# Weight quantisation moved from the second feed-forward into six slots of the first attention

## The reference, cut to what matters

```python
x = x + 0.5 * L0_ffn(layernorm(x))
x = x + L0_attn(layernorm(x))       # 16 heads of 8, banded bias
x = x + 0.5 * L0_ffn(layernorm(x))
x = x + 0.5 * L1_ffn(layernorm(x))  # FP4: the weights w_gate, w_up, w_down are quantised
x = x + L1_attn(layernorm(x))
x = x + 0.5 * L1_ffn(layernorm(x))

def fp4_quant_dequant(x):           # blocks of 16 along the last dimension
    scale = max(abs(block)) / 6
    q = nearest_grid_value(abs(x / scale)) * sign(x) * scale
```

## Time and profile before

| | |
|---|---|
| median of 3 runs | 506.68 us (506.49 to 509.33) |
| the profiled execution's own time | 506.44 us |
| its span in the profile | 504.6 us |
| PE busy | 418.7 us (83%) |
| DVE busy | 350.3 us (69%) |
| ACT busy | 285.1 us (56%) |
| POOL busy | 305.0 us (60%) |
| mean granted clock of TensorE | 0.91 |

### The profile page before, as it was taken

The page is one execution under the profiler, slowest core; times in us unless marked ns, Lnnn a source line. Parts: engine busy times, 40 slices in busy tenths (PEclk is TensorE's granted clock), DMA queues, the critical chain, the costliest instruction groups (busy, mean ns, idle before and its releaser), DMA issues.

```text
span 504.6 us, 11467 instructions
## 1 busy us (share of the span) xinstructions
PE 418.7 (83%) x3693; PEld 268.9 (53%) x3693; DVE 350.3 (69%) x882; ACT 285.1 (56%) x521; POOL 305.0 (60%) x585
## 2 busy tenths in 40 slices
PE   3996889999999967685788478799999998767975
PEld 1453425666666643343456355567766765334654
DVE  5769686888778644874899637857676776148992
ACT  5774515666666755657885135235455546668741
POOL 5314336777777770546898325346666677679961
PEclk9999957999999999987999679759999999579997
DMA  6001793332333000000000004973323330000001
GB/s 196 1 2 47 173 271 82 96 97 76 85 82 96 5 2 0 2 0 1 1 1 2 1 0 136 254 182 91 86 78 89 95 97 3 2 2 0 22 21 43
DMA packets 31122, 31.77 MB, mean 63 GB/s; under 512 B 4954, under 2 KB 26330, under 8 KB 31075
## 3 DMA queue, kind: packets, MB, share of 16 engines
q1 hardware_dynamic: 31074, 31.18, 23.2%
HBM read 21.30 MB, written 9.44 MB: 61 GB/s over the span
## 4 chain that ended last, share of the span: by engine, by line
PE 53%; DVE 14%; POOL 13%; issue 10%; ACT 6%; DMA 2%; SPq 1%; DVEq 0%; POOLq 0%; ACTq 0%
PE psum L639 6%; PE psum L293 4%; POOL hq L1175 4%; PE psum L593 3%; PE psum L623 3%; POOL hb_v L1170 3%; PE psum L594 2%; PE psum L596 2%; DVE nm L729 2%; PE psum L613 2%; PE psum L643 2%; DVE nm L732 2%; DVE xn L228 2%; PE psum L614 2%; PE psum L416 2%
## 5 line engine op out<-in xcount | busy, mean ns | idle before, releaser
L688 ACT ACTIVATE h_sb<-psum 128x1024 f32<-128x1024 f32 (+1 forms) x128 | 110.7, 914 | 52.8 <-PE psum L614 26.8
L729 DVE TENSOR_REDUCE nm<-psum 128x2 f32<-128x512 f32 x128 | 82.3, 685 | 14.0 <-PE psum L594 12.8
L732 DVE TENSOR_REDUCE nm<-psum 128x3 f32<-128x384 f32 x128 | 65.7, 552 | 11.3 <-PE psum L600 9.3
L698 POOL TENSOR_TENSOR h_sb<-h_sb,bandw 128x512 f32<-128x512 f32 x48 | 61.0, 1270 | 0.0
L234 POOL TENSOR_TENSOR rstd<-veps,mhalf 128x4 f32<-128x4 f32 (+1 forms) x32 | 28.3, 884 | 45.0 <-DVE veps L220 43.6
L639 PE MATMUL psum<-h_sb,v_b 128*32 128x256 f32 x512 | 44.0, 416 | 4.2 <-POOL h_sb L698 4.1
L766 DVE RECIPROCAL rsum<-psum 128x16 f32<-128x16 f32 x32 | 8.2, 258 | 49.7 <-PE psum L655 49.7
L702 POOL TENSOR_SCALAR_AFFINE_SELECT h_sb<-h_sb 128x512 f32<-128x512 f32 x64 | 40.8, 638 | 0.0
L593 PE MATMUL psum<-kst,qst 72*128 72x256 bf16 x128 | 36.0, 298 | 3.4 <-DVE nm L729 2.5
L596 PE MATMUL psum<-kst,qst 72*128 72x128 bf16 x128 | 30.2, 236 | 7.8 <-DVE nm L732 6.5
L594 PE MATMUL psum<-kst,qst 72*128 72x256 bf16 x128 | 36.1, 298 | 0.0
(11 more groups left out here) (234 smaller groups left out, 1158.3 us busy)
## 6 DMA issues: line engine op xcount, KB each, us to landing
qst<-q_dram SPq DMA_DIRECT2D x96, 96.0 KB
kst<-k_dram SPq DMA_DIRECT2D x96, 96.0 KB
q_dram<-q_parts SPq DMA_DIRECT2D x16, 192.0 KB, 3.2
k_dram<-k_parts SPq DMA_DIRECT2D x16, 192.0 KB, 3.5
k_dram<-k_parts SPq DMA_DIRECT2D x16, 128.0 KB, 3.6
x<-in_L_attn_x SPq DMA_DIRECT2D x4, 256.0 KB, 4.5
out_x<-x SPq DMA_DIRECT2D x4, 256.0 KB, 2.3
pk<-in_packed SPq DMA_DIRECT2D x1, 689.5 KB, 5.8
```

The costliest lines, as they stand in the source:

```text
L688: nc.scalar.activation(pexp[p][:, :, 0:w], psum[:, 4 + 2 * (p % 2):6 + 2 * (p % 2), 0:w], ACT.Exp, scale=scale).then_inc(sem("a_exp"), 1)
L698: ins = nc.gpsimd.tensor_tensor(wide, wide, bandw[:].unsqueeze(1).unsqueeze(1).to_broadcast([P, 2, 2, P]), ALU.mult)
L729: nc.vector.tensor_reduce(nm[slot % 2][:, HEAD[h]], bank[e].rearrange("p (t k) -> p t k", t=2), AX.X, ALU.max, negate=True).then_inc(sem(" ...
L732: nc.vector.tensor_reduce(nm3[slot % 2][:, HEAD[h]], bank[e][:, 0:3 * P].rearrange("p (t k) -> p t k", t=3), AX.X, ALU.max, negate=True).t ...
```

## The change

The entry `quantise` of `ffn_b` becomes empty. `unit` gets a hook that is called at its beginning, after DVE's second pair of maxima, and at its end. In the opening quad the hook handles matrices 0 and 1, in slots 0 and 1 of the final quad matrix 2. In an even slot DVE does steps 0 to 3 after its second pair and POOL does `weight_v_pool` at the end of the slot; in an odd slot DVE does steps 5 to 7 and POOL `weight_pool`. The second attention has no such calls.

```diff
-            def unit(eng, which, qd, slot, has_prev, has_prev2, has_1, has_2, has_3):
+            def unit(eng, which, qd, slot, has_prev, has_prev2, has_1, has_2, has_3, extra=lambda point: None):
+                extra("begin")
...
                     if has_2:
                         dve_max(eng, *n2, 1)
+                    extra("max1")
+                    if has_2:
                         dve_max(eng, *n2, 2)
                     if has_prev:
                         dve_norm(eng, *prev)
...
+                extra("end")
...
+        def weights_beside(eng, which, n, point):
+
+            c = n // 2
+            if (which, point) == ("dve", "max1"):
+                for k in ((0, 1, 2, 3), (5, 6, 7))[n % 2]:
+                    weight_step(eng, c, k)
+            if (which, point) == ("pool", "end"):
+                (weight_v_pool, weight_pool)[n % 2](eng, c)
...
-                           ("pe", 1): [("a_y", 8), ("a_exp", PR * 16)]}, {4: 0, 5: 1, 6: 2})
+                           ("pe", 1): [("a_y", 8), ("a_exp", PR * 16)]}, {})
...
+            def attention_with_weights(at, beside):
+                def opening(slot, point):
+                    weights_beside(eng, which, slot, point)
+
+                def final(slot, point):
+                    if slot < 2:
+                        weights_beside(eng, which, 4 + slot, point)
+
+                for n in (0, 1, 3):
+                    at["quad"](eng, which, n, beside, final=final, opening=opening)
+                at["back"](eng, which)
...
-            attention(attn_a, next_ffn)
+            attention_with_weights(attn_a, next_ffn)
```

More of the change, by code:

```diff
@@ L14 @@
 import numpy as np
+from functools import partial
 import concourse.bass as bass
@@ L910, in front, with quad @@
                     pool_split(eng, q0, slot)
-            def quad(eng, which, n, beside):
+            def quad(eng, which, n, beside, final=lambda slot, point: None, opening=lambda slot, point: None):
                 if which == "sp" and n < 2:
@@ L918, in quad @@
                     for slot in range(4):
-                        unit(eng, which, q0, slot, slot > 0, slot > 1, True, True, True)
+                        unit(eng, which, q0, slot, slot > 0, slot > 1, True, True, True, partial(opening, slot))
                 elif n == 1:
@@ L926, in quad @@
                         beside(slot)
-                        unit(eng, which, q0 + 3, slot, True, True, slot < 3, slot < 2, slot < 1)
+                        unit(eng, which, q0 + 3, slot, True, True, slot < 3, slot < 2, slot < 1, partial(final, slot))
             def back(eng, which):
```

## The result

The changed kernel takes **516.2 us** (median of 4 runs, 514.4 to 520.4) against 507.7 us (506.5 to 509.3) for the kernel before in the same comparison: ratio **1.0171**, 95% interval 1.0123 to 1.0219. It is slower by 8.5 us; forecast were 2.2, and 516.2 lies above the range. The profiled execution took 515.4 us with a span of 513.6, 9.0 more than before, at a mean granted clock of 0.891 against 0.910.

A forecast was written before the change was run, and what follows sets the result against it. TensorE was taken to bound the first attention, DVE the second feed-forward. Saving - 6.7, DVE's inserts + 6.7, POOL's pieces + 0.5 and tail + 1.75 gave + 2.2 us: 508.9 us, range 503.3 to 512.3.

The forecast's parts named there:

- The saving: Second feed-forward: without the weights its two long steps shrink to those of the first feed-forward, 6.7 us gone.
- The mechanism of the inserts: First attention: a DVE tensor_scalar from SBUF to SBUF waits for the POOL instruction in progress, 0.47 us on average.
- D = 2.2 us: First attention: length of one DVE insert, 1.3 us with POOL silent, two waits for POOL adding 0.93.
- The tail of the change: End of the first attention: POOL's pieces for the third matrix delay the last masks, passed on whole, 1.75 us.
- POOL's pieces in slots and tail: First attention: POOL's added instructions cost 0.5 us in the slots and 1.75 us at the attention's end.
- Together 6.7 us for DVE: First attention: six DVE inserts, less the idle time covering them, delay PE by 6.7 us; bounds 2.0 to 11.0.
- the wait of PE at the attention's end was there before: Argument against a low-clock loss in the second feed-forward: PE already waited 3.12 us on the last masks.
- rival 3: Second feed-forward's saving isn't collected, PE starting at a low clock, or opening slots stay at 0.50; 512 us; chance 0.07.
- Rival 1: First attention: the inserts run undisturbed in POOL's gaps, 1.3 us each; 504.3 us; chance 0.28.
- rival 4: The first attention swallows all the added work, tail included; 500.0 us; chance 0.05.
- rival 2: First attention: every insert meets POOL at its worst, 2.9 us long, and DVE bounds the slots; 513.3 us; chance 0.15.
- L989 might grow by 0.47 us: Third rounding step, a DVE tensor_tensor, might also wait for POOL: 1.4 us over three inserts, forecast then 510.3.

The follow-up runs named there:

- dve_reduce: The changed kernel without POOL's weight instructions, each of DVE's weight instructions replaced by a reduction of about its length; 505.9 us, ratio 0.9950.
- dve_only: The changed kernel with only DVE's seven instructions per matrix, on the raw weights, POOL's three left out; 516.8 us, ratio 1.0172.
- end: The changed kernel with DVE's pieces moved from between the second and third pair of maxima to their slot's end; 505.5 us, ratio 0.9963.
- pool_only: The changed kernel with only POOL's three instructions per matrix, DVE's seven left out; 506.1 us, ratio 0.9952.
- before_2: The kernel before, unchanged, run once more for a second profile; one run of 511.9 us.
- none: The changed kernel with the quantisation of the weights left out altogether; 509.2 us (median of 6), too scattered for a ratio.
- reorder: The kernel before with POOL's last two weight products and DVE's rounding steps moved later in the second feed-forward; 502.2 us, ratio 0.9864.
- end_late: The changed kernel with DVE's pieces at their slots' ends and POOL's last piece moved from final slot 1 to final slot 3's end; 508.9 us, ratio 0.9981.
- after_warm: The changed kernel with fourteen spare bf16 products of 128x512 on PE in the first attention's last slot; 516.4 us, ratio 1.0166.

## Why the prediction was wrong

**Right.** The saving: 6.7 us forecast, 6.3 in the change and 6.8 with no weights at all. The mechanism of the inserts: a tensor_scalar from SBUF to SBUF waits for POOL's product, shown by `dve_reduce` against `dve_only` (1.3 against 8.3 us at nearly the same lengths) and by `end` against the change. D = 2.2 us, measured 2.3 on average. The tail of the change: 1.75 us forecast, 1.75 measured as the hold of the masks; final slot 1 to the end grew by 1.7 us in all. POOL's pieces in slots and tail: 2.25 forecast, 2.2 in `pool_only`; but that the sum fits is luck, since by the starts of the normalisations in `pool_only` the last opening slot and the first of the loop lost 1.1 us (forecast 0.5) and the tail 1.1 (forecast 1.75).

**Mis-sized: the term of DVE's inserts, "Together 6.7 us for DVE".** It measured 8.3. Of `dve_only` against before, counted from the first maximum by the starts of the normalisations, slots 0 and 1 lost 1.9 us (forecast 1.3), slot 2 2.4 (1.36), slot 3 1.5 (1.36), final 0 and 1 1.0 and 1.4 (1.36 each). The final slots are as forecast or cheaper; the excess of 1.8 us is in the opening, where slots 0 and 1 have the longest insert (3.0 us) and slot 2 lost 1.1 us more than forecast though its insert took only 2.1 us. Between the normalisations of slots 1 and 2 lies the fall of the clock from 1.00 to 0.52 that follows PE's wait on the slot 1 insert: the term passed the delay on to PE at full clock and had no price for the clock that a delay takes down with it. With reductions in the same place the clock stayed at 1.00 and slot 2 lost 0.1 us. No run held the clock fixed, so how the 1.1 us divide between clock and delay is not shown. 8.3 lies inside the bounds that the prediction gave for this term, 2.0 to 11.0.

**Failed: "Against: the wait of PE at the attention's end was there before." By this step rival 3 got only 0.07.** The low clock at the start of the feed-forward is an effect of its own, 3.6 us on top of the forecast, and it came at the tile I had said I would leave as it is. It comes with a longer attention: all seven profiles without the products whose attention was over 1 us longer took 10.97 to 12.40 us to tile 1's `s_sb`, all four whose attention kept its length (before, before_2, none, reorder) 8.83; `pool_only`, 2.2 us longer and without one insert, is among the seven, and so is `end_late`, whose projections took the same 30.79 us as those of `before_2` and `none`. PE's wait on the last masks had not grown (3.12 us in the change; in `pool_only` and `end` it was even shorter, 1.83 and 0.31 us, behind longer waits on the masks of slot 2, 2.44 and 2.91 against 0.97 in before). So not the length of the last wait decides, but where the waits fall; `after_warm` shows that PE's idling is the cause at that place (8.83 with the products), and its unchanged total that this clock time isn't simply won back. What fixes the place is open.

**Sum.** Forecast + 2.2; + 1.6 for the larger insert term (8.3 less 6.7) and + 3.6 for the clock ahead of tile 1 give + 7.4. The interval of the ratio is 6.2 to 11.1 us, and 7.4 lies inside it, as the measured 8.5 does; in the profiled execution another 1.7 us fell before the attention, by chance as far as the runs tell. Taking the 3.6 us away with the products did not shorten the whole, so this term is read from the stretches and not shown in the total. Rival 1 and rival 4 are excluded by D = 2.3 and by the tail; rival 2's price was reached in opening slot 1 alone (3.0 us).

By the Trainium skill (SBUF — State Buffer, Who interferes with whom) a DVE instruction with two SBUF inputs contends with a POOL instruction that reads SBUF, and issue order decides who waits. The prediction had held by it that L989 might grow by 0.47 us. In `after` it kept 0.57 us, and the POOL product issued 0.12 us behind it took 1.58 instead of 1.26: the trace agrees with the order, and the price was POOL's, where the mask had room.

## What to carry to other kernels

Before work is moved into another stage's idle time, look at which engine's instruction runs at that very point: the same seven instructions per matrix cost 8.3 us in the middle of POOL's products, and the whole change came out level with the kernel before, or 0.4% ahead (0.9963, 0.9930 to 0.9995), once they stood where POOL had short steps. Price a delay by the chain it stands in (PE's scores behind DVE's maxima), and add a case for the clock wherever the delayed stretch starts or ends with PE waiting, even if that wait is already there before. And try first whether the collision that makes the old place expensive goes away by reordering it there: that gave 1.2 to 1.4% and had no second half to pay for.

## What the runs showed of the hardware

- One DVE step may wait for a POOL product many times its own length: 128x24 elements, 0.18 us alone, took 0.87 to 0.98. Reductions of the same length, and reciprocals (0.29 to 0.30 us), kept theirs beside POOL.
- It works in both directions: POOL's 128x8 product took 0.31 instead of 0.20 us while L985's wait ended (87.30), and its 128x512 one 1.58 instead of 1.26 behind L989.
- After PE's wait of 3.1 us the clock of `after` stayed at 0.50 or little above until 216 us, though PE was busy 4.83 of 5.69 us in the last step of it. In `before`, after the same wait, it was back at 1.00 by the last normalisation (192.24 us).
- A wait of PE of one and the same length can leave the clock alone or take it down: 2.21 us in the projections of `before` left it at 1.00, and behind 2.22 us at the same instructions of `after` it was 0.80 over 52 to 56 us. Between the fourteen profiles the outcome went with the time at which the stretch began.
- Fourteen spare products narrowed the range of the kernel before from 505 to 515 us down to 504 to 509 us.
